# Two projections of a fused attention and mixture layer, cut into 64-row halves that run in pairs on TensorE

## The reference

```python
h = layernorm(x) * (1 + ca) + sa
qkv = h @ w_qkv.T + b_qkv                       # q, k, v: 16 heads of 16
scores = einsum('bhqd,bhkd->bhqk', q, k) / 4 + alibi_causal_mask
x = x + ga * (softmax(scores) @ v) @ w_out.T + ...
h = layernorm(x) * (1 + cb) + sb
p = softmax(h @ gate_W.T)                       # 8 experts
x = x + gb * (sum over experts of count * p * (h @ expert_W[e].T)) @ out_W.T
```

## Time and profile before

| | us |
|---|---|
| median of 3 runs (lowest, highest) | 1567.94 (1562.91, 1567.96) |
| span of the profiled execution, first to last instruction | 1560.2 |
| PE busy in it | 1472.0 (94%) |
| DVE busy | 1277.9 (82%) |
| ACT busy | 1147.2 (74%) |
| POOL busy | 858.0 (55%) |

### The profile page before, as it was taken

The page is one execution under the profiler, slowest core; times in us unless marked ns, Lnnn a source line. Parts: engine busy times, 40 slices in busy tenths (PEclk is TensorE's granted clock), DMA queues, the critical chain, the costliest instruction groups (busy, mean ns, idle before and its releaser), DMA issues.

```text
span 1560.2 us, 56229 instructions
## 1 busy us (share of the span) xinstructions
PE 1472.0 (94%) x21476; PEld 946.3 (61%) x21476; DVE 1277.9 (82%) x3030; ACT 1147.2 (74%) x2464; POOL 858.0 (55%) x924
## 2 busy tenths in 40 slices
PE   6888999999999999999999999999999999999996
PEld 5555656666666666666666666656666656666653
DVE  6777888888888888888888888888888888888836
ACT  2477777778777777777877877777777777777762
POOL 2124556556556556655655665565665565566454
PEclk9799999999999999999999999999999999999988
DMA  5344555555455555455555545555545555554521
GB/s 170 99 150 127 171 156 173 152 170 157 149 178 155 175 153 166 143 168 167 157 180 152 160 146 170 166 160 157 165 142 167 175 150 178 154 169 139 157 73 50
DMA packets 197298, 239.73 MB, mean 154 GB/s; under 512 B 22462, under 2 KB 147782, under 8 KB 197030
## 3 DMA queue, kind: packets, MB, share of 16 engines
q1 hardware_dynamic: 196972, 236.07, 49.4%
q10 hardware_dynamic: 64, 0.07, 0.0%
HBM read 134.25 MB, written 100.73 MB: 151 GB/s over the span
## 4 chain that ended last, share of the span: by engine, by line
PE 62%; DVE 10%; DMA 9%; issue 6%; SPq 6%; ACT 3%; POOL 2%; POOLq 0%; DVEq 0%; ACTq 0%
PE ps L599 26%; PE ps L753 11%; PE ps L748 8%; PE ps L807 6%; DMA qk_d<-qk_st 5%; PE ps L802 5%; DVE mxp L1089 3%; DMA kz<-qk_d 2%; PE ps L768 2%; PE ps L662 2%; SPq L412 2%; DVE ve_c L1014 1%; DVE zr L1101 1%; DVE st_c L1000 1%; SPq L429 1%
## 5 line engine op out<-in xcount | busy, mean ns | idle before, releaser
L1089 DVE TENSOR_REDUCE mxp<-ps 128x4 f32<-128x512 f32 (+1 forms) x1536 | 842.8, 592 | 160.5 <-PE ps L768 155.6
L863 ACT ACTIVATE prob<-ps 128x512 f32<-128x512 f32 (+1 forms) x1536 | 732.6, 525 | 121.8 <-PE ps L753 116.4
L753 PE MATMUL ps<-qs,kz 50*128 50x128 f16 (+2 forms) x3584 | 405.9, 240 | 12.9 <-DVE mxp L1089 10.5
L768 PE MATMUL ps<-kz,qs 49*128 49x128 f16 (+1 forms) x4096 | 410.5, 231 | 0.1
L753 PEld LDWEIGHTS ps<-qs,kz 50*128 50x128 f16 x3584 | 261.4, 94 | 88.7 <-ACT prob L863 31.1
L768 PEld LDWEIGHTS ps<-kz,qs 49*128 49x128 f16 x4096 | 286.3, 95 | 3.8 <-DVE mxp L1089 1.8
L1347 POOL TENSOR_TENSOR om<-oc,rz 128x512 f32<-128x512 f32 x62 | 77.4, 1270 | 329.9 <-DMA rz<-rz_d 329.9
L807 PE MATMUL ps<-prob,va 128*32 128x384 f32 (+2 forms) x3072 | 237.6, 381 | 0.0
L748 PE MATMUL ps<-mk 64*128 64x256 bf16 x1024 | 198.6, 274 | 36.0 <-DMA kz<-qk_d 11.3
L802 PE MATMUL ps<-prob,va 128*32 128x128 f32 x4096 | 209.6, 277 | 0.6 <-DVE qk_st L1021 0.6
L764 PE MATMUL ps<-mk 64*128 64x256 bf16 x1024 | 201.0, 276 | 5.4 <-DVE mxp L1089 3.4
(11 more groups left out here) (157 smaller groups left out, 2870.6 us busy)
## 6 DMA issues: line engine op xcount, KB each, us to landing
qk_d<-qk_st SPq DMA_DIRECT2D x128, 256.0 KB, 2.8
ou_d<-ou SPq DMA_DIRECT2D x124, 256.0 KB, 2.3
qs<-qk_d SPq DMA_DIRECT2D x256, 96.0 KB, 2.4
kz<-qk_d SPq DMA_DIRECT2D x256, 96.0 KB, 2.5
xa<-in_L_attn_x SPq DMA_DIRECT2D x32, 512.0 KB, 5.2
qk_d<-qk_st SPq DMA_DIRECT2D x128, 128.0 KB, 3.4
xc<-in_L_attn_x SPq DMA_DIRECT2D x32, 512.0 KB, 4.1
oc<-ou_d SPq DMA_DIRECT2D x31, 512.0 KB, 4.9
```

Source lines behind the costliest of these rows:

```text
L753: x_ = mm(bank[:, col:col + w * P], kz[rows, h // 2, kt * P:(kt + 1) * P], qs[rows, h // 2, qt * P:(qt + w) * P], start=(n > 0), stop=(n > ...
L768: x_ = mm(bank[:, col * P:(col + w) * P], qs[rows, h // 2, qt * P:(qt + 1) * P], kz[rows, h // 2, kt * P:(kt + w) * P], start=(n > 0), sto ...
L863: nc.scalar.activation(prob[:, h % 8, at:at + w], ps[:, ST + n, 0:w], ACT.Exp, scale=1.0 / FS).then_inc(s["exp_done"], 1)
L1089: v.tensor_reduce(mxp[:, g % 2, at, first:first + apart * (BLOCKS[n] - 1) + 1:apart], bank.rearrange("p (m k) -> p m k", k=P), AX.X, ALU.m ...
```

## The change

`qk` for n = 0 and n = 1 is replaced by `qk_halves`. It computes the same two outputs in two passes of twelve matmuls. Each matmul has 64 contraction rows. In pass 0, q's bank takes channels 0 to 63 of each chunk (array rows 0 to 63) and k's bank channels 64 to 127 (rows 64 to 127), alternately; pass 1 takes the other halves and adds them. Both banks are complete only after pass 1. Pass 0 stays at slot 4, place 0; pass 1 goes to slot 4, place 1, with 4.0 between them. The readers and the `t2` steps move too.

```diff
-    4: [(0, "qk", 0, 1), (0, "qk", 1, 1), (1, "t2", 0, -2)],
-    5: [(1, "t2", 1, -2), (1, "v", 0, 1)],
+    4: [(0, "qk", 0, 1), (1, "qk", 1, 1)],
+    5: [(0, "t2", 0, -2), (1, "t2", 1, -2), (1, "v", 0, 1)],
...
-    4: [(0, "qk_hi", 0, 1), (0, "qk_hi", 1, 1), (1, "hf_c", 0, -2), (1, "hh_c", 0, -2), (2, "hf_c", 1, -2),
-        (3, "hh_c", 1, -2)],
-    5: [(2, "negm", 2, 0)],
+    4: [(1, "qk_hi", 0, 1), (1, "qk_hi", 1, 1), (3, "hf_c", 0, -2)],
+    5: [(0, "hh_c", 0, -2), (1, "hf_c", 1, -2), (2, "hh_c", 1, -2), (2, "negm", 2, 0)],
...
-    4: [(0, "qk_lo", 0, 1), (1, "qk_lo", 1, 1), (1, "invert", 0, -1)],
+    4: [(1, "qk_lo", 0, 1), (1, "qk_lo", 1, 1), (1, "invert", 0, -1)],
...
+            def qk_halves(b, n):
+
+                wait(pe, "hla_ready", (b + 1) * 2)
+                at = (to("qk", 0, b), to("qk", 1, b)) if n == 0 else (ps[:, bank_of("qk", 0, b), :], ps[:, bank_of("qk", 1, b), :])
+                if n:
+                    wait(pe, "qk_half", (b + 1) * 2)
+                for c in range(DC):
+                    for m, (w_, h_) in enumerate(((wqkv_hi, hh_a), (wqkv_hi, hl_a), (wqkv_lo, hh_a))):
+                        first, last = (c, m) == (0, 0), (c, m) == (DC - 1, 2)
+                        for j in range(2):
+                            half = slice(HALF * (j ^ n), HALF * (j ^ n) + HALF)
+                            x_ = mm(at[j], w_[half, c, j * D:j * D + P], h_[half, c, :], start=(n == 0 and first),
+                                    stop=(n == 1 and last))
+                            if last:
+                                x_.then_inc(s["qk_ready" if n else "qk_half"], 1)
...
-                qk(b, n)
+                if (b, n) == (0, 0):
+                    pe.wait_ge(s["set_dve"], WQKV)
+                if n < 2:
+                    qk_halves(b, n)
+                else:
+                    qk(b, n)
```

More of the change, by code:

```diff
@@ L275, in build @@
                      "xa_loaded", "lna_stats", "lna_aggr", "lna_ready", "rsa_ready", "xna_ready",
-                     "ta_ready", "hfa_ready", "hha_ready", "hla_ready", "qk_ready", "qk_hi", "qk_lo",
+                     "ta_ready", "hfa_ready", "hha_ready", "hla_ready", "qk_ready", "qk_half", "qk_hi", "qk_lo",
                      "qk_stored0", "qk_stored1", "qk_stored2", "qk_stored3", "stack_loaded0", "stack_loaded1",
@@ L672, in qk @@
             def qk(b, n):
-                if (b, n) == (0, 0):
-                    pe.wait_ge(s["set_dve"], WQKV)
                 dst = to("qk", n, b)
```

## The result

The changed kernel takes 1625.23 us (median of 5 runs, 1619.64 to 1626.39) against 1565.16 (5 runs, 1558.94 to 1567.96): a ratio of 1.0374, interval 1.0348 to 1.0400. It is 60 us slower; the prediction said 1620 and slower at 0.90. The profiled execution has a span of 1624.6 us, 64.4 above that of before; it is the slowest of the five (1626.39).

What follows compares the result with a forecast made beforehand. PE was taken to bound nearly everywhere, with the transfers last at slot 8 by 0.64 us. PE's 2.40 less 0.64 gives 1.76 us over 29 laps; with 1 us for first laps, 1567.9 + 52 = 1620 us, range 1588 to 1640.

Steps and rivals of the forecast that it cites:

- PE's products, changes of height, weight loads: Projections on PE: pairs 0.215 us apart, array time unchanged; two height changes go, 0.20 us less; doubled weight loads cost nothing.
- the rival in which the full-height products expose their loads: Projections before the change expose 0.10 us per product, so halves save it: 1584 us; chance 0.01, inside another rival's.
- Readers: Evictions of q and k through t2, hh_c and gate: q whole only after all halves; PE reaches slot 8 2.40 us later.
- Only the transfers are late: Rival at slot 8: looser order around v 0 to gate leaves about 0.52 us a lap; 1584 us, chance 0.13.
- more is lost: Rival: gate's delay also delays its DVE steps and exponentials of slots 6 and 7; 2.5 us a lap, 1641 us, chance 0.10.
- serial pairs: Rival at the projections: 512-column pairs take 0.43 us, not 0.215; 2.6 us a lap on top, 1701 us, chance 0.02.
- faster: Rival: 4.0 between passes feeds ACT and DVE earlier and height changes go; 0.3 us a lap gained, 1559 us, chance 0.07.
- The first rival: Same as "Only the transfers are late": PE's net delay at slot 8 comes to about the transfers' 0.52 us; chance 0.13.
- The sum: Whole span: 29 laps at 1.76 us give 51 us, with the first laps +52 us, 3.3%.
- the first lap's: Laps 0 and 1 and before the first, without t2: v 0 waits for q's low part instead; 1 us.
- The slack at slot 8: Before the change the transfers arrive 0.64 us a lap after PE, so PE's delay is free up to that.
- the transfers' own delay: Slot 8: the inversion starts 0.52 us later, so the transfers' arrival moves by 0.52 us, below PE's own delay.

Runs made afterwards that it cites:

- full_moved: The changed kernel with all its moved steps, but q and k made by full-height products again; 1617.4 us, ratio 1.0318.
- first_full: The changed kernel, but for the first batch q and k are made by full-height products; 1622.78 us, ratio 1.0346.
- rz_late: The kernel before, with SP's store of the inverted sums put behind the stores of the first q and k; 1568.02 us, ratio 1.0001.
- halves_only: The kernel before, with the two passes of halves back to back at slot 4, place 0, nothing else moved; 1598.32 us, ratio 1.0189.
- hh_first: The changed kernel, but ACT writes hh_c 1 ahead of the exponential of slot 5's part 1; 1592.24 us, ratio 1.0164.
- full_hh: The changed kernel with full-height products for q and k, and hh_c 1 ahead of the exponential of slot 5's part 1; 1571.03 us, ratio 1.0017.
- loads_moved: The kernel before, with the 512 KB loads of xa and xc moved away from the stores of the first q and k; 1548.55 us, ratio 0.9878.
- after_rz_late: The changed kernel, with SP's store of the inverted sums put behind the stores of q and k; 1625.33 us, ratio 1.0359.

## Why the prediction was right

Times from the last score piece of slot 3, the walk of the prediction against one lap of the trace:

| step | forecast | measured |
|---|---|---|
| pass 0, pass 1 start | 0.11, 1.85 | 0.12, 1.86 |
| t2 0 starts (its wait) | 4.84 (1.22) | 4.89 (1.23) |
| inversion starts | 5.38 | 5.41 |
| v 0 starts (its wait) | 7.03 (0.44) | 7.09 (0.40) |
| hh_c 1 ends | 10.19 | 10.19 |
| gate starts | 11.49 | 11.57 |
| slot 8 starts | 18.3 | 18.35 |

*PE's products, changes of height, weight loads:* as said; the row behind the doubled loads held (PEld 4.0 us busier in all, nothing of it exposed), and the rival in which the full-height products expose their loads fell with it: full_moved has them again, and they start 0.217 us apart.

*Readers:* PE's own arrival at slot 8 moved by 2.49 us (18.35 against 15.65 + 0.21 from the same origin) where the walk had 2.40. The undisturbed laps split it: 0.54 for the halves (47.76 - 47.22), 1.33 for the place of `hh_c` 1 (47.76 - 46.43), and 0.60 for the place of k's product and of the readers (45.87 - 45.27), each shown by a run; together 2.47. Less the slack and with what slots 8 to 3 add (both below), 2.49 - 0.79 + 0.13 = 1.83 of the 1.84 us that a lap lost. "Only the transfers are late", "more is lost", "serial pairs" and "faster" fell.

The first rival was priced below its own terms: 1.22 + 0.36 - 0.20 - 0.64 is 0.74 us, not about 0.52. It fell anyhow, since `hh_c` 1 behind exponential 5.1 cost what the walk said.

*Sizes that were off.* The sum was 52 us; the medians differ by 60, the profiles by 64.4. By the profiles: 28 laps from the first `gate` are 59.5 us longer (1345.2 against 1285.7), where undisturbed laps alone give 28 x 1.84 = 51.5; four laps hold 7.6 us more and the others 0.4. The forecast had no term for TensorE's clock. A stretch of the changed kernel, at a mean granted clock of 0.63:

```profile
211.00:214.50 3.50, 2.76 (x17) 1.53 (x15) 1.00 (x3) 1.28 (x3) 0.87 (x2) 0.63 0.87 290
```

It lies in one of those four laps; none of the 28 laps of the kernel before has such a stretch. Then, before lap 2's `gate`, 5.8 us are lost, 2.5 of them that lap's own delay, 3.3 the first lap's, which I had put at 1: first_full shows 1.6 of them at the first row scores, but not that they last until that `gate`; the rest is open. The slack at slot 8 was 0.79 us by the timelines, not 0.64: the sum of waits leaves out those that the view puts down to another releaser, and starts each 0.07 us late, at the end of the last product (762.98 + 0.38) and not where the next piece could have started (762.98 + 0.31). Against that, from slot 8 to the next end of slot 3 a lap takes 29.40 us (801.05 to 830.45) instead of 29.16 (763.89 to 793.05; 29.28 in the mean of 27 laps, so 0.13 more). I had that stretch unchanged. That ACT and DVE catch up in the kernel before while PE waits for the transfers, and after can't, would explain it; no run shows it. And the transfers' own delay was 0.02 us, not 0.52: the walk took their landing to hang on the moment of their issue, and rz_late shows that it doesn't. It decided nothing here, because PE's chain ended last by far; that this step was wrong and the forecast wasn't is luck.

*Still open:* why some laps lose the clock and others with the same waits don't. It comes with crowded waits (none of 28 laps in the kernel before and in halves_only, which has one long wait a lap; 10 in full_moved, five stretches each in the changed kernel and in hh_first), yet full_hh and loads_moved have one among their laps too, and after_rz_late and first_full, with every wait of the changed kernel, have one stretch each against its five. So the same waits cost the clock in one execution and not in another, and no run filled a wait with work to show the cause.

## What to carry to other kernels

A product that is cut so that two outputs grow together is as long as before for PE, but its first output is ready only at the end; count from the first reader, not from the product, and follow that reader's chain to the last engine. In an in-order queue one producer of a long chain placed behind an instruction that waits for the other engine can cost the whole wait (1.3 us a lap here, for one entry of a table). A delay that hides behind a transfer isn't gone: full_hh and the kernel before take the same time with PE 0.60 us apart. Ask of each large load near a critical store whether it is needed then: moving two that weren't gave what no change of the order of stores did.

## What the runs showed of the hardware

TensorE's clock fell to its lower level for short stretches in the middle of a kernel that is 91% busy on PE, behind waits of 1.2 us and less, and cost 8 us in the changed kernel and 14 in full_moved. Pairs of 64-row matmuls with 512 columns run fully side by side, 0.215 us apart. And issuing stores 0.86 us earlier landed them no earlier while the DMA engines were full (busy share 0.95 to 1.05); with two loads of 512 KB taken away from there (0.55, then 0.02) they landed 1.09 us earlier. What had to be moved at the time counted, not the moment of issue.
